# How many products stand behind each group of counts in a two-layer graph network: six and seven in turn instead of eight

## What is computed

```
def _L0_gnn_ref(...):
    msg = (node_states[src] + rel_emb[edge_type_ids]) @ W_msg.T + b_msg
    agg = segment_sum(msg, dst) / max(deg, 1)
    return node_states @ W_self.T + b_self + agg
def sage_conv(x, src, dst, W_l, W_r, b, n):
    return segment_mean(x[src], dst, n) @ W_l.T + b + x @ W_r.T
x = layernorm(x + L0(x))
h = silu(sage_conv(x, W1_l, W1_r, b1))
x = layernorm(x + sage_conv(h, W2_l, W2_r, b2))
```

## Time and profile before

| | |
|---|---|
| median of 3 runs | 361.33 us (360.99 to 362.14) |
| profiled execution, its own time | 361.31 us |
| its span | 359.5 us |
| TensorE matmul / weight load | 330.7 us (92%) / 243.8 us (68%) |
| VectorE | 231.5 us (64%) |
| ScalarE | 171.5 us (48%) |
| GpSimd | 4.9 us (1%) |
| mean DMA rate | 19 GB/s |

### The profile page before, as it was taken

How to read it: one execution, slowest core, us unless ns; L and a number is a source line. 1 busy time by engine, 2 the same in 40 slices (tenths; PEclk the granted TensorE clock), 3 DMA queues, 4 the chain that set the end, 5 groups by cost and what they waited for, 6 DMA issues and landing times.

```text
span 359.5 us, 9075 instructions
## 1 busy us (share of the span) xinstructions
PE 330.7 (92%) x3335; PEld 243.8 (68%) x3335; DVE 231.5 (64%) x596; ACT 171.5 (48%) x380; POOL 4.9 (1%) x18
## 2 busy tenths in 40 slices
PE   0699899999999999999999999999999999999970
PEld 0688798998998989989964455455474455455460
DVE  6999999989989989999447930330254031440454
ACT  3685567778778778687422151132151141122040
POOL 5000000000000000000000000000000000000000
PEclk9999999999999999999999999999999999999996
DMA  4711000000000000001100000000000001101102
GB/s 144 228 39 54 2 2 5 2 2 4 2 2 3 2 3 4 3 2 31 37 7 1 2 0 2 0 0 2 0 2 1 2 0 30 31 0 31 30 0 68
DMA packets 6580, 6.97 MB, mean 19 GB/s; under 512 B 593, under 2 KB 5510, under 8 KB 6534
## 3 DMA queue, kind: packets, MB, share of 16 engines
q1 hardware_dynamic: 6246, 5.92, 5.6%
q10 hardware_dynamic: 288, 0.43, 0.4%
HBM read 4.75 MB, written 1.60 MB: 18 GB/s over the span
## 4 chain that ended last, share of the span: by engine, by line
PE 79%; DVE 6%; ACT 3%; issue 2%; ACTq 0%; DVEq 0%
PE ps L996 36%; PE ps L980 17%; PE ps L925 14%; PE ps L1067 5%; PE ps L1077 3%; PE ps L1011 1%; ACT counts L870 1%; DVE hot L1229 1%; PE ps L932 1%; PE ps L942 1%; ACT scaled L826 1%; DVE new_first L1354 1%; DVE table L1239 1%; DVE hot L1222 0%; DVE table L1229 0%
## 5 line engine op out<-in xcount | busy, mean ns | idle before, releaser
L996 PE MATMUL ps<-counts,table 128*128 128x512 f16 (+1 forms) x750 | 136.2, 340 | 0.0
L870 ACT CAST counts<-ps 128x494 f32 x208 | 107.5, 579 | 44.2 <-PE ps L925 43.7
L996 PEld LDWEIGHTS ps<-counts,table 128*128 128x128 f16 x750 | 62.0, 97 | 68.6 <-issue 0.2
L925 PE MATMUL ps<-hot 128*128 128x156 f16 (+1 forms) x592 | 67.7, 237 | 14.3 <-DVE hot L1229 13.5
L980 PE MATMUL ps<-counts,table 128*128 128x256 f16 x600 | 78.2, 271 | 0.0
L925 PEld LDWEIGHTS ps<-hot 128*128 128x128 f16 x592 | 52.2, 100 | 17.8 <-DVE hot L1229 15.2
L1229 DVE TENSOR_TENSOR hot<-iota,edges 128x1200 f16<-128x1200 f16 x74 | 57.5, 777 | 0.0
L980 PEld LDWEIGHTS ps<-counts,table 128*128 128x128 f16 x600 | 53.0, 97 | 5.6
L1222 DVE TENSOR_TENSOR hot<-iota,edge_rows 128x768 f16<-128x768 f16 x74 | 40.8, 551 | 2.8 <-PE ps L962 2.3
L932 PE MATMUL ps<-window_hot,hot 128*128 128x19 f16 x296 | 42.2, 177 | 0.0
L1319 DVE TENSOR_TENSOR new_first<-ps,scaled 128x512 f32<-128x512 f32 (+1 forms) x9 | 5.4, 600 | 54.0 <-ACT scaled L826 54.0
(11 more groups left out here) (139 smaller groups left out, 324.0 us busy)
## 6 DMA issues: line engine op xcount, KB each, us to landing
own_T<-x_turned SPq DMA_DIRECT2D x4, 256.0 KB, 2.6
table<-x_rows SPq DMA_DIRECT2D x1, 832.0 KB, 6.0
table<-x_rows SPq DMA_DIRECT2D x1, 768.0 KB, 4.2
out<-new_first SPq DMA_DIRECT2D x3, 256.0 KB
out<-hot SPq DMA_DIRECT2D x3, 256.0 KB, 2.4
sum_first<-x_turned SPq DMA_DIRECT2D x2, 256.0 KB, 4.6
counts<-first_dst ACTq DMA_DIRECT2D x1, 208.0 KB, 3.5
counts<-dst_t SPq DMA_DIRECT2D x1, 208.0 KB, 4.5
```

The source lines that it names most:

```text
L870: nc.scalar.copy(A[:, HALVES[half], bass.ds(bases[group % 8], GROUP_W)], window(group, half)).then_inc(copied[half], 1)
L925: return nc.tensor.matmul(window(group, half)[:, :, at[t]], row(tiles[t], LOW_AT, P), blocks_of(tiles[t], half), start=group == half == t ...
L996: last = nc.tensor.matmul(ps[:, sums_bank(q), 0:nodes], table[:, b, which, :], A[:, b, at:at + nodes], start=b == which == 0, stop=b + 1 = ...
```

## The change

```
@@ spread() @@
     for group in range(GROUPS):
-        room = 0 if group in OWN else 8
+        room = 0 if group in OWN else 6 + group % 2
         if waiting and waiting[0][0] <= group:
             k, cost, some = waiting.pop(0)[1:]
             room -= cost
```

## The result

| | before | changed |
|---|---|---|
| median, profiled execution and timed runs | 361.16 us (360.98 to 362.14, 4 runs) | 357.01 us (356.80 to 357.67, 4 runs) |
| profiled execution, its own time | 361.31 us | 357.20 us |
| its span | 359.5 us | 355.3 us |

The ratio is 0.9883 with a 95% interval of 0.9865 to 0.9902: 1.2% faster, 4.15 us between the medians. The forecast was 357.3.

A forecast was written before the change was run, and what follows sets the result against it. Loop bound by TensorE in groups with eight products, by ScalarE in those with none. Work 128.2 plus new waits 2.5 gives 130.7 against 134.7 us, 4.0 off 361.33: 357.3 us, range 355.4 to 360.3.

The forecast's parts named there:

- The place: End of layer 0's last full-chunk products: kernel time moves by what this moves, from 181.9 to 177.9 us.
- The work: TensorE's work from group 21's release to the last full-chunk products' end: 127.1 us before, 128.2 after.
- The 1.1 us for ten products deferred: Groups 11 to 20, paced by VectorE, take 56 products instead of 66; the ten left over cost 1.1 us.
- The waits that went: Loop groups with no products, mainly where parts end: all 7.6 us of old waits taken as gone.
- The waits that came: New waits in the loop from evacuation, scaling and VectorE, put at 2.5 us together.
- The evacuation: First product of every second part waits for ScalarE to evacuate the finished sum: 0.25 us five times, 1.2.
- The scaling: ScalarE's 1.0 us message scaling between two pairs of copies delays TensorE 0.13 us, four times, 0.5.
- VectorE: 0.8 was put in: Thinner VectorE lead with one-hots during chunk bursts: 0.8 us, chosen between nothing and 2.0 over four chunks.
- A: Rival: VectorE's bursts eat its lead, TensorE waits 1.0 us in four chunks, not 0.2; 359.5 us, chance 0.15.
- B: Rival: hand-over waits at five places stay 1.1 to 1.2 us each, so no gain; 361.3 us, chance 0.09.
- C: Rival: no new wait shows in the loop; 354.8 to 355.9 us, chance 0.08.
- D: Rival: VectorE paces the whole loop, 18 products moved behind it lie bare, 2.0 us slower; 363.3, chance 0.08.

The follow-up runs named there:

- e1: Kernel before with room for 4 products instead of 8 in groups 99 to 103, moving 20 products behind the loop: 361.65 us.
- e5: Changed kernel with room for 8 products up to group 20 and 5 in groups 21 to 27, putting back the ten deferred products: 356.07 us.
- e2: Kernel before, product table unchanged, with ScalarE's normalising done two tiles at a time and its high part later, out of the empty groups: 360.20 us.
- e3: Changed kernel with room for 7 products in every group, leaving 1 product in a chunk's last group instead of 4 or 5: 359.00 us.
- e9: Changed kernel with a chunk's degrees counted one group earlier, ahead of the product that waits for ScalarE's evacuation: 356.48 us.
- e11: As e10, with ScalarE scaling a chunk's messages two tiles at a time behind two groups instead of all four behind one: 354.33 us.
- e10: Changed kernel with more room in early groups, seven products in each chunk's last group, and degrees moved as in e9: 355.13 us.
- e6: Changed kernel with a useless VectorE reduction of about 0.7 us behind the measuring of each of the first four chunks: 357.30 us.
- e4: Changed kernel with sixes and sevens reordered in groups 21 to 95, giving the last group of a chunk's second part 7 products: 356.81 us.

## Why the prediction was right, step by step

**The place.** "The time of the kernel moves by what the end of part 11 moves": forecast 177.9, measured 177.72, with 177.6 us behind it in both kernels. From the release of group 21 it is 130.4, where 130.7 was forecast.

**The work.** 0.73 a group, 0.112 a product inside and 0.11 behind the loop all come back in the changed trace. e1 shows by itself that a product costs the same on either side of the loop. The first pair of node products with the degrees, put at 0.73, takes 0.65 in the changed kernel, so some 0.3 of waiting had been counted as work. The 1.1 us for ten products deferred out of the groups that VectorE paces is 0.94 by e5.

**The waits that went.** All of them were taken as gone, and line 942 has left the list of waits. e2 shows what they were made of where parts ended: at group 61 0.38 of 1.04 was the piece of normalising, and the rest was the evacuation and copies that need 0.92 where counts need 0.73. The prediction put down all of them to ScalarE. At groups 35 and 69 that was wrong: 0.9 of the 7.6 was TensorE's own load of positions with no product to hide it. The change removes it by the same means, so the number didn't suffer. The 0.9 that the prediction read as TensorE's waits for one-hots was this load too, which speaks still more for its view that VectorE had room.

**The waits that came** were put at 2.5 and are about 2.5, but the shares differ, and that the sum fits is partly luck: one term too small and one left out made up for one that isn't there.
- The evacuation: 0.25 x 5 = 1.2 forecast. By the distance from a release to the next group's first count, less the products, the five are 0.30, 0.37, 0.28, 0.39 and 0.27, 1.6 in all. The term was mis-sized since 1.45, the end of the evacuation's row, was taken for the moment at which TensorE starts; the weights of the first product are loaded 1.56 after the release. e3 has the same 1.56 with one product ahead of it, and e9 puts work into the wait without moving that product's group.
- The scaling: 0.13 x 4 = 0.5 forecast. The counts of groups 34, 51, 68 and 85 take 0.10 to 0.16 longer, about 0.5 in all. e11 takes this away, and gains 0.8 on e10, where the same waits are 0.75.
- VectorE: 0.8 was put in and the stretch has nothing of it. The one wait of 0.3 stands ahead of the release of group 21. Behind it the lead goes down to 0.5 us at group 92 but never to nothing. This term was wrong.
- Left out: the counts of groups 46, 80 and 98 take 0.07, 0.10 and 0.24 longer, 0.4 in all. ScalarE is not the cause, as its copies are done in time and line 942 doesn't wait. In group 98 there is a gap of TensorE's own (timeline of its weight loads):

```profile
161.28 0.10 PEld L925 LDWEIGHTS ps<-table 128*128 128x128 f16 x1 [0.15 <-issue]
```

Each of these groups comes right behind a load of positions with little work to cover it (it started at 160.2 here and took 0.59). That this load is the cause is likely but no run shows it.

**The rivals.** A (VectorE's bursts) is refuted by e6: 3.0 us more of them cost 0.3 to 0.4. B (the hand-over only changes its name) is refuted in size: 0.3 a place, not 1.1 to 1.2. C would have been 354.8 to 355.9; the waits are there. D (VectorE sets the pace, products bare behind the loop) is refuted by the result, in which the loop did get shorter, and its price by e1. With it falls what was drawn from the Trainium skill, Perfetto Trace Analysis, section Identifying the Most-Contended Engine: VectorE had the highest occupancy by that reading and has it still (97.4 against 93.6), and yet the time went with TensorE's order. The same page of the Trainium skill says under Optimization Strategy that regimes with different most-contended engines may gain from being interleaved. The trace agrees with that: in the empty group 61 (107.36 to 109.13) ScalarE was busy all of 1.77 us and TensorE's weight loads 0.88, in the groups of eight from 66 to 81 us ScalarE 11.4 of 15.0 and the weight loads 13.9 (VectorE 14.0), and mixing the two brought the 4.2 us.

**Still open.** About 0.1 a place at five hand-overs in e10 and e11, and the gaps at groups 46, 80 and 98. A second bank for the sums should remove the chain of e4, but the loop leaves none of the eight free, and no run tries it.

## What to carry to other kernels

When a filler is spread over a loop, the sum of the work says nothing of the gain. Look for the iterations in which the filler is absent and ask which other engine then sets the pace, or which step of the engine's own the filler was hiding (here a load of positions); even rations pay by what is held up there. A view of waits names the work that ended last in the record and can name the wrong engine, so check it against when the data was ready. Then cost the hand-over that the even rations bring close together (last use of a bank, evacuation, first use), by the start of the next instruction and not by the end of the evacuation's row, and put small independent work into it. In this kernel an occupancy of 97% on another engine was no bound, because its lead, read as the distance from its result to the use, never went to nothing.

## What the runs showed of the hardware

In some executions TensorE's granted clock falls for a few microseconds early in the loop, where it is still waiting for VectorE. The windows of e6's profiled execution (18 to 24 us) and of the changed kernel's (18 to 22 us):

```profile
18.00:20.00 2.00, 1.49 (x23) 1.12 (x20) 1.88 (x4) 2.00 (x5) 0.00 (x0) 1.00 0.03 8
20.00:22.00 2.00, 1.71 (x17) 1.73 (x18) 1.45 (x4) 1.92 (x5) 0.00 (x0) 0.52 0.00 0
22.00:24.00 2.00, 2.00 (x19) 1.94 (x19) 1.41 (x4) 0.36 (x1) 0.00 (x0) 0.62 0.00 0
```
```profile
18.00:20.00 2.00, 1.53 (x23) 1.16 (x20) 1.89 (x5) 2.00 (x5) 0.00 (x0) 1.00 0.03 8
20.00:22.00 2.00, 1.66 (x21) 1.56 (x22) 1.76 (x5) 2.00 (x5) 0.00 (x0) 1.00 0.00 0
```

In the first the mean clock of 20 to 22 us is 0.52 of full speed and of 22 to 24 us 0.62, so most of both was at 1.2 GHz; in the second it stays at 1.00, 2.4 GHz. TensorE was busy 1.49 and 1.53 of 2.00 in the 2 us ahead, and in neither case was it idle for long. Group 21 is released 1.2 us later in e6 (48.50 against 47.34), and the execution took 358.79 where the other three took 357.20 to 357.36. The profiled executions of e1 and e11 have it too, so part 11 starts late in the trace of e11 (171.02) though its median is the lowest. The distances in the table of the experiments start behind it. What decides it from one execution to the next no run here shows.
